# The inverse's steps moved between the gate products and beside the turns, and the out-projection in one piece

## The reference

```python
mixed = x @ w_qkv; z = (x @ w_z)                  # 16 heads of k and q, 32 of v and z, each 128 wide
mixed = silu(causal_conv4(mixed)); q, k, v = split(mixed)
q, k = l2norm(q) * DK ** -0.5, l2norm(k)
for t in range(512):                              # for each batch row and head
    S = S * exp(g[t])
    delta = (v[t] - k[t] @ S) * beta[t]
    S = S + outer(k[t], delta)
    o[t] = q[t] @ S
out = rmsnorm(o * silu(z)) * norm_w @ w_out       # summed over the heads
```

## Time and profile before

| | |
|---|---|
| median of 3 runs | 3194.74 us (3192.93 to 3197.19) |
| the profiled execution | 3209.77 us, span 3208.0 us |
| TensorE matmuls, weight loads | 2896.3 us (90%), 2387.1 us (74%) |
| VectorE, ScalarE, GpSimd | 2720.8 (85%), 1854.5 (58%), 627.8 us (20%) |
| attention part | about 91 to 2780 us of the span |

### The profile page before, as it was taken

One profiled execution on the slowest core, in us unless ns is written; L12 is line 12 of the kernel. 1 busy time (PEld: TensorE's weight loads), 2 busy tenths in 40 slices (PEclk: granted clock), 3 DMA queues, 4 the chain that ended last, 5 costly groups with the idle time before them and its releaser, 6 DMA issues. The chain is left out here.

```text
span 3208.0 us, 78521 instructions
## 1 busy us (share of the span) xinstructions
PE 2896.3 (90%) x28584; PEld 2387.1 (74%) x28584; DVE 2720.8 (85%) x6189; ACT 1854.5 (58%) x6002; POOL 627.8 (20%) x911
## 2 busy tenths in 40 slices
PE   6899999999999999999999999999999999638999
PEld 3787878787778877777878787878777777526665
DVE  3798988888888888898989898889888888779984
ACT  3566656565666566666666665656666655443332
POOL 1121212121212111121212121112121211053320
PEclk9899999999999999999999999999999999858999
DMA  6433433333433333434333333334343333120000
GB/s 246 139 82 97 115 101 108 99 109 101 115 92 102 101 115 93 115 91 118 95 109 84 101 115 100 109 100 112 97 115 83 109 102 95 19 96 20 24 17 17
DMA packets 571685, 309.46 MB, mean 96 GB/s; under 512 B 401699, under 2 KB 532899, under 8 KB 553638
## 3 DMA queue, kind: packets, MB, share of 16 engines
q1 hardware_dynamic: 571302, 304.43, 33.5%
HBM read 243.07 MB, written 50.73 MB: 92 GB/s over the span
## 5 line engine op out<-in xcount | busy, mean ns | idle before, releaser
L1070 DVE SCALAR_TENSOR_TENSOR conv<-xb,convw,conv 128x512 f32<-128x512 f32 x768 | 596.1, 780 | 101.6 <-ACT conv L784 86.8
L574 PE MATMUL bank<-x_hi,w_hi 128*128 128x512 f32 x1024 | 431.2, 421 | 11.2 <-PEq L263 6.3
L574 PE MATMUL bank<-x_hi,w_lo 128*128 128x512 f32 x1024 | 403.9, 394 | 0.0
L574 PE MATMUL bank<-x_lo,w_hi 128*128 128x512 f32 x1024 | 401.6, 392 | 0.0
L778 ACT ACTIVATE xb<-bank 128x512 f32<-128x512 f32 x256 | 161.1, 629 | 304.7 <-PE bank L574 279.9
L586 PE MATMUL bank<-w_hi,x_hi 128*128 128x256 f32 x1024 | 307.4, 300 | 24.0 <-ACT conv L784 24.0
L586 PE MATMUL bank<-w_lo,x_hi 128*128 128x256 f32 x1024 | 292.2, 285 | 0.2 <-issue 0.2
L586 PE MATMUL bank<-w_hi,x_lo 128*128 128x256 f32 x1024 | 292.3, 285 | 0.0
L1153 POOL TENSOR_TENSOR small<-small,half 128x4 f32<-128x4 f32 x64 | 64.5, 1008 | 1080.8 <-DVE small L901 1080.8
L1181 POOL COPY halo<-xb 128x12 f32<-128x12 f32 x256 | 88.2, 345 | 917.7 <-ACT xb L778 917.7
L559 PE MATMUL bank<-wout_hi,onT_hi 128*128 128x512 f32 x512 | 227.0, 443 | 43.8 <-issue 23.0
(11 more groups left out here) (268 smaller groups left out, 7688.6 us busy)
## 6 DMA issues: line engine op xcount, KB each, us to landing
x_hi<-x_hi_scratch SPq DMA_DIRECT2D x63, 1024.0 KB, 5.0
x_lo<-x_lo_scratch SPq DMA_DIRECT2D x63, 1024.0 KB, 7.3
E<-decay_scratch SPq DMA_DIRECT2D x64, 512.0 KB, 5.4
M_scratch<-M SPq DMA_DIRECT2D x128, 256.0 KB, 2.4
w_raw<-in_w_proj SPq DMA_DIRECT2D x64, 384.0 KB, 8.5
Uf<-U SPq DMA_DIRECT2D x640, 16.0 KB, 1.9
w_raw<-in_w_out SPq DMA_DIRECT2D x32, 256.0 KB, 3.4
Mt<-M_scratch SPq DMA_DIRECT2D x256, 32.0 KB, 1.9
```

Of the source, the lines that this page charges most:

```text
L574: mm = pe.matmul(banks[j % 2][:].rearrange("p (b t) -> p b t", b=B), lhsT=t[f"w_{p}"][:, k, j, :], rhs=t[f"x_{q}"][:, k], start=i == 0, st ...
L1070: dve.scalar_tensor_tensor(out=y3, in0=xb[:, :, i:i + C], scalar=t["convw"][:, j, i:i + 1], in1=y3, op0=ALU.mult, op1=ALU.add).then_inc(on ...
```

## The change

Only the order of calls changes, on three engines; no instruction is added or removed, and no DMA is moved in SyncE's program. On TensorE `gate` 3 is no longer cut in two; the four steps of the solve stand between the gates, `join_a` and `join_b` beside the turns, and the 24 out-projection matmuls behind all of it. On ScalarE the second gate silu comes before the turns, `turn` is split by head, the joins stand between its halves, and the silus of v come last. On VectorE the taps of v follow the solve's steps, and the four small transposes that read Y leave `y_part` 1 and become `turn_Y`, behind `turn` 0.

```diff
 TensorE
                 gate(r + 2, 0)
+            if solve:
+                x_part(r + 1, 0)
+            if ahead:
                 gate(r + 2, 1)
+            if solve:
+                y_part(r + 1, 0)
+            if ahead:
                 gate(r + 2, 2)
             if solve:
-                x_part(r + 1, 0)
-            if ahead:
-                gate(r + 2, 3, range(0, 6))
+                x_part(r + 1, 1)
+            if ahead:
+                gate(r + 2, 3)
+            if solve:
+                y_part(r + 1, 1)
             if state:
                 turn(r, 0)
             if solve:
-                y_part(r + 1, 0)
-            if ahead:
-                gate(r + 2, 3, range(6, 12))
+                join_a(r + 1)
             if state:
                 turn(r, 1)
             if solve:
-                x_part(r + 1, 1)
-            if state:
-                out(r, 0, 0)
-                out(r, 1, 0)
-            if solve:
-                y_part(r + 1, 1)
-            if state:
-                out(r, 0, 1)
-                out(r, 1, 1)
-            if solve:
-                join_a(r + 1)
-            if state:
-                out(r, 2, 0)
-                out(r, 2, 1)
-            if solve:
                 join_b(r + 1)
             if state:
-                out(r, 3, 0)
-                out(r, 3, 1)
+                for pair in ((0, 1), (2, 3)):
+                    for j in range(HJ):
+                        for b in pair:
+                            out(r, b, j)
 ScalarE
             if ahead:
-                silu(r + 2, 2)
-            if state:
-                turn(r)
+                gate(r + 2, 1)
+            if state:
+                turn(r, 0)
+            if solve:
+                join_a(r + 1)
+            if state:
+                turn(r, 1)
+            if solve:
+                join_b(r + 1)
...
             if ahead:
-                gate(r + 2, 1)
+                silu(r + 2, 2)
             if fresh:
                 split(r + 3, 3)
-            if solve:
-                join_a(r + 1)
             if ahead:
                 silu(r + 2, 3)
-            if solve:
-                join_b(r + 1)
 VectorE
+        def turn_Y(s):
+            y8 = blocks8(solve_bank(1))
             for q in (0, 2):
                 dve.transpose(U[rows(q), 0:4, rows(q + 1)], y8[rows(q + 1), 0:4])
                 op = dve.transpose(U[rows(3 - q), 4:8, rows(2 - q)], y8[rows(2 - q), 4:8])
...
                 factors(r)
+            if solve:
+                turn_T(r + 1, 0)
             if ahead:
                 taps(r + 2, 1, range(early, TAPS - 1))
-                taps(r + 2, 2)
-            if solve:
-                turn_T(r + 1, 0)
+            if solve:
                 x_part(r + 1, 0)
             if ahead:
-                taps(r + 2, 3, (0,))
+                taps(r + 2, 2, (0,))
             if solve:
                 y_part(r + 1, 0)
-            if state:
-                turn(r, 0)
-            if solve:
                 turn_T(r + 1, 1)
                 x_part(r + 1, 1)
+            if ahead:
+                taps(r + 2, 2, (1,))
+            if solve:
+                y_part(r + 1, 1)
+            if state:
+                turn(r, 0)
+            if solve:
+                turn_Y(r + 1)
             if state:
                 turn(r, 1)
-            if solve:
-                y_part(r + 1, 1)
+            if ahead:
+                taps(r + 2, 2, (2,))
             if state:
                 out(r, 0)
             if ahead:
-                taps(r + 2, 3, (1, 2))
+                taps(r + 2, 3, (0, 1))
             if state:
                 out(r, 1)
             if ahead:
+                taps(r + 2, 3, (2,))
                 decays(r + 2)
```

More of the change, by code:

```diff
@@ L576, in project, with gate @@
             mm.then_inc(on["proj"], 1)
-        def gate(s, b, terms=range(len(TERMS))):
+        def gate(s, b):
             half, i = divmod(b, 2)
@@ L583, in gate @@
                 pe.wait_ge(on["w_lo"], 6 * (s // NC))
-            for n in terms:
-                k, p, q = TERMS[n]
+            for n, (k, p, q) in enumerate(TERMS):
                 mm = pe.matmul(banks[half][:, i * 256:(i + 1) * 256], lhsT=t[f"x_{p}"][:, k, b, :], rhs=t[f"w_{q}"][:, k, 4:6, :],
@@ L615, in tensor @@
                 gate(r + 2, 0)
-                gate(r + 2, 1)
-                gate(r + 2, 2)
             if solve:
@@ L620, in tensor @@
             if ahead:
-                gate(r + 2, 3, range(0, 6))
+                gate(r + 2, 1)
+            if solve:
+                y_part(r + 1, 0)
+            if ahead:
+                gate(r + 2, 2)
+            if solve:
[4 more added lines that the diff above has]
+                y_part(r + 1, 1)
             if state:
@@ L751, in normed, with turn @@
                 op.then_inc(on["on"], 1)
[L753 to L759, removed]
+        def turn(s, j):
+            act.wait_ge(on["on_turned"], 2 * s + j + 1)
+            if s:
+                act.wait_ge(on["out_proj"], 4 * s)
+            act.activation(t["onT_hi"][:, j].rearrange("p b s -> p (b s)"), banks[6 + j][:], ACT.Copy,
+                           scale=t["normw"][:]).then_inc(on["onT_hi"], 1)
         def split_wout(h, j):
@@ L1116, in vector @@
                 factors(r)
+            if solve:
+                turn_T(r + 1, 0)
             if ahead:
                 taps(r + 2, 1, range(early, TAPS - 1))
-                taps(r + 2, 2)
             if solve:
-                turn_T(r + 1, 0)
                 x_part(r + 1, 0)
             if ahead:
-                taps(r + 2, 3, (0,))
+                taps(r + 2, 2, (0,))
             if solve:
                 y_part(r + 1, 0)
+                turn_T(r + 1, 1)
+                x_part(r + 1, 1)
+            if ahead:
+                taps(r + 2, 2, (1,))
+            if solve:
+                y_part(r + 1, 1)
             if state:
@@ L1129, in vector @@
             if solve:
-                turn_T(r + 1, 1)
-                x_part(r + 1, 1)
+                turn_Y(r + 1)
             if state:
                 turn(r, 1)
-            if solve:
-                y_part(r + 1, 1)
+            if ahead:
+                taps(r + 2, 2, (2,))
             if state:
```

## The result

The changed kernel takes 3325.4 us (median of 4 runs, 3317.2 to 3329.2) against 3196.0 before in the same comparison: 1.040 times as long, 95% interval 1.038 to 1.042. The forecast was 3315, range 3235 to 3385. The profiled execution has a span of 3327.4 us.

What follows compares the result with a forecast made beforehand. Neither TensorE nor VectorE alone was the bound, but a serial chain through the inverse with DMA round trips. 16 x (2.5 + 3 x 1.0) = 88 us plus 32 for the clock, 120 on 3194.7, gave 3315, range 3235 to 3385.

Steps and rivals of the forecast that it cites:

- x_part waits for Tc: TensorE, first x_part: moved ahead of gates 1 and 2, it idles 2.5 us until the Tc load lands.
- From y_part to the turns: First y_part to next turns: 15.05 us against 12.2, +2.9, as join_b and the out block wait for VectorE's transposes.
- Taps behind the transposing of Tc: VectorE, chunk 1's step: y_part 3.1 us sooner, -0.2 against the later part's +2.9; same value for chunks 2 and 3.
- VectorE's tail: VectorE's last sums end 3.4 us after the turns start instead of 2.2; chain 0.9 to 1.2 us later, chunks 1-3.
- SyncE's freer queue: Uf loads issued earlier no longer stand against M's store: 0 to 1.5 us sooner in chunk 3, about 0.5 in chunk 2.
- Chunk 2: Chunk 2's step was given the value of chunks 1 to 3: -0.2 + 1.2 = +1.0 us.
- The clock: Gate product behind x_part's long wait runs at the lower clock, 1.0 us more in chunks 0 and 3: 32 us.
- Rival 2: TensorE's clock falls in all 64 steps, in the second half too: 173 us more, 3368; chance 0.15.
- Silu, counted as nothing: ScalarE's v silus, put last, cost nothing as ScalarE idles 42%; if that cover were gone, 0.7 us a step.
- The sum of 120 us: Whole kernel: 88 us from the four chunks' steps over 16 heads, plus 32 for the clock.
- the step of 42.3 us for chunk 0: Sign to look for in the profile after: the step of chunk 0 takes near 42.3 us.

Runs made afterwards that it cites:

- e1: Changed kernel with VectorE's turn_Y (the four small transposes that read Y) put back ahead of turn 0; 3262.7 us, ratio 1.020.
- e2: Changed kernel with the first six out matmuls between turn 1 and join_b on TensorE; 3260.5 us, ratio 1.020.
- e7: Kernel before, with taps of v behind Tc's transposing and v silus last in chunks 1 and 2, turn 0 behind first y_part in all; 3159.8 us.
- e3: Changed kernel with VectorE's decay scan ahead of its first out sum; 3297.7 us, ratio 1.032.
- e4: Changed kernel computing gate product 1 once more ahead of the first x_part in chunks 0 and 3; 3317.4 us, ratio 1.038.
- e6: Changed kernel with gates 0 and 1 before x_part, out-projection split, turn_Y not behind a turn's round trip, decay scan earlier; 3211.0 us, ratio 1.004.
- e10: e6 with ScalarE's last silu of v moved behind the next step's lengths; 3165.1 us, ratio 0.9905.
- e5: Changed kernel with gate 1 back ahead of the first x_part, gates 2 and 3 following x_part and the first y_part; 3371.4 us, ratio 1.054.

## Why the prediction was right

- *x_part waits for Tc.* Right: 2.17 us in the step shown, 2.6 in the mean of chunk 0 and 2.5 in chunk 3, 2.5 forecast. In chunk 0 Tc lands 24.7 us after the turns, before 25.2.
- *From y_part to the turns.* Right in its parts: `join_b` waits 1.34 us (1.30 forecast for the transposes), the out block takes 5.6 us (5.7). The whole is 15.3 us in the median against 15.05, but 15.6 in the mean: +3.4 in each of the 64 steps where +2.9 was forecast. e1 and e2 each took the wait away and got 63 and 65 us. This is the largest term.
- *Taps behind the transposing of Tc.* Right, and e7 shows it as a gain by itself. `y_part` comes 2.4 us sooner in chunk 1 with the tail's delay in it; forecast -3.1 + 1.2 = -1.9.
- *VectorE's tail.* Right: 3.6 us after the turns (3.4), M 0.95 us later in chunks 1 and 3 and 1.2 in chunk 2 (0.9 to 1.2). e3 took it back and gained 28.
- *SyncE's freer queue.* The prediction named it (0 to 1.5 us in chunk 3) but gave it no term in the sum; it is larger. In chunk 3 M starts 0.95 later and yet N lands 1.4 us sooner (13.6 after the turns against 15.0), and Tc 1.9 sooner. No run moved the Uf loads alone, so that the queue did this is read from the traces, not tested.
- *Chunk 2* was mis-sized: the prediction gave it chunk 1's value, +1.0, and it measured +1.9. Its first `y_part` had been less late before (30.6 against 31.1) and waited 0.16 us for Xc where chunk 1's waited 1.21, so there was less to gain; the trace had that row.
- *The clock.* Half right. Chunks 0 and 3 hold 29 of the 32 stretches at the lower clock, 24 of them in or right behind `x_part`'s wait, in 31 steps. From the first `x_part` to `y_part` took 3.0 us in the mean of chunk 0 and 3.3 in chunk 3, against 2.3 in e4's chunk 3, where no such stretch is left: 0.7 and 1.0 us lost, 1.0 forecast in both. Rival 2 doesn't hold: in chunks 1 and 2 `x_part` waits 0.7 us in the mean and at most 1.9, and no stretch begins right behind it. The case in the Trainium skill ("TensorE: Matmul & The Clock Gate", section "HAM oscillation — how this bites in real kernels") is a loop whose wait in each pass is longer than its matmuls, which no step here is, so the prediction stretched its rule when it carried it to all 64 steps.
- *Silu, counted as nothing.* Wrong, hidden by other delays: in the changed kernel VectorE's first instruction on the lengths starts 0.24 us later in chunk 0; in e6 the same order cost 2.3 us a step there.
- The sum of 120 us came within 9 of the measured 129 in part by luck, as errors offset each other: chunk 0 +3.2 (3.5 with the clock), chunk 1 +1.1 (1.0), chunk 2 +1.9 (1.0), chunk 3 +1.7 (2.0). In chunk 0 the part to `y_part` was forecast 0.65 longer and came 0.3 shorter, the part behind 2.9 longer and came 3.5. Of the signs, the step of 42.3 us for chunk 0 came at 43.4; it leaves out the clock's 1.0 that the sum has.

## What to carry to other kernels

Before work is moved to fill small waits, look at what it covers where it stands: the gate products that ended just as a DMA landed were cover, and so were the out matmuls spread through VectorE's chain. In an order written by hand a group in one piece is a wait with no cover ahead of it. And the engine that looks idle (ScalarE, 56%) can hold the chain with one instruction that waits for a late tap in front of one that is wanted at once; reordering by what is due first brought 46 us (e10), moving the taps of v behind one transposing in two of four chunks 39 (e7, with turn 0 and the silus reordered).

## What the runs showed of the hardware

Computing a product twice (31 x 1.44 us of added work, e4) cost no time that can be told, and left 7 instead of 24 stretches at the lower level (1.2 GHz) behind `x_part`'s wait, in one profile of each. In e5 two waits of 1.8 and 1.05 us with only small matmuls between them stood in every step, and in 39 places a stretch at the lower level begins between the second `y_part`'s wait and the end of the out block; in the step shown it covers nine out matmuls. In the changed kernel `x_part` 1, `y_part` 1, `join_a` and `join_b` wait 0.2 (0.6 in chunk 1), 0.2, 0.4 and 1.35 us (medians), with a gate product ahead of the second `y_part`, and 6 of the 61 steps have such a stretch in that place.
